# Threshold search by marks, sums on TensorE and two groups, with the weight quantisation on VectorE in its gaps

## The reference, cut to what matters

```
# layer 0, per batch: h = ctx (512 x 128), x' = layernorm(x)
sim = sum over heads of Q K^T / (sqrt(32) * 4)          # 512 x 512
k = int(512 * 0.3)                                      # 153
threshold = top_k(sim, k)[0][:, -1:]                    # the k-th largest of each row
A = sigmoid(sim) * (sim >= threshold)
A = (A + A^T) * 0.5
x = x + tanh(g_xattn[0]) * ((1 - gamma) * x' + gamma * A)
# layer 1: weights w_gate, w_up (2048 x 512), w_down (512 x 2048) are quantised in
# blocks of 32 (shared power of two, 1-bit mantissa, saturation at 6), then
out = (silu(q(z) @ q(w_gate)^T) * (q(z) @ q(w_up)^T)) quantised, @ q(w_down)^T
# layers 2 and 3 (attention; top-2 of 8 experts) are not touched
```

## Time and profile before

| | |
|---|---|
| median of 3 runs | 2155.13 us (2154.55 to 2155.16) |
| profiled execution, its time | 2153.45 us |
| its span on the core | 2151.7 us, mean granted TensorE clock 0.83 |
| DVE busy | 1576.6 us (73%) |
| PE busy | 1449.3 us (67%) |
| ACT busy | 959.3 us (45%) |
| POOL busy | 426.4 us (20%) |

### The profile page before, as it was taken

The page is one execution under the profiler, slowest core; times in us unless marked ns, Lnnn a source line. Parts: engine busy times, 40 slices in busy tenths (PEclk is TensorE's granted clock), DMA queues, the critical chain, the costliest instruction groups (busy, mean ns, idle before and its releaser), DMA issues.

```text
span 2151.7 us, 32048 instructions
## 1 busy us (share of the span) xinstructions
PE 1449.3 (67%) x10939; PEld 922.7 (43%) x11014; DVE 1576.6 (73%) x2526; ACT 959.3 (45%) x1591; POOL 426.4 (20%) x325
## 2 busy tenths in 40 slices
PE   4000051113767776889999770999999999999990
PEld 2000040012333332444444370677777777777760
DVE  4999999997888887888888453466666666666634
ACT  5787811123232223555545332455555555555520
POOL 3000003243000000666767606000000000000006
PEclk8555575556888887999999855899999999999995
DMA  9000030100000000000000007666666666666617
GB/s 354 9 0 0 0 118 0 78 0 25 0 0 0 0 0 0 2 1 2 2 2 1 2 0 273 226 227 233 227 225 232 227 226 229 229 227 229 228 61 234
DMA packets 86470, 222.09 MB, mean 103 GB/s; under 512 B 7424, under 2 KB 7680, under 8 KB 85888
## 3 DMA queue, kind: packets, MB, share of 16 engines
q1 hardware_dynamic: 80752, 204.37, 27.8%
q0 software_dynamic: 5120, 16.78, 2.3%
q10 hardware_dynamic: 528, 0.02, 0.0%
HBM read 184.44 MB, written 36.70 MB: 103 GB/s over the span
## 4 chain that ended last, share of the span: by engine, by line
PE 47%; DVE 7%; issue 4%; POOL 2%; ACT 0%; DMA 0%; POOLq 0%; DVEq 0%; ACTq 0%; SPq 0%
PE PS L1527 23%; PE PS L1546 11%; PE PS L1164 3%; DVE R L1017 2%; PE PS L1140 2%; PE PS L1150 2%; PE PS L1125 2%; DVE R L989 2%; PE PS L1139 1%; POOL R L1696 1%; PE PS L1412 1%; PE PS L1507 1%; PE PS L1115 1%; PE PS L1404 1%; DVE R L1021 1%
## 5 line engine op out<-in xcount | busy, mean ns | idle before, releaser
L1527 PE MATMUL PS<-R 128*128 128x256 f16 x4416 | 499.1, 273 | 1.1 <-ACT R L1583 1.1
L1527 PEld LDWEIGHTS PS<-R 128*128 128x128 f16 x4416 | 431.8, 98 | 66.8 <-issue 1.4
L1546 PE MATMUL PS<-R 128*128 128x512 f16 x1104 | 253.3, 379 | 0.2 <-DVE R L1656 0.2
L1234 DVE SCALAR_TENSOR_TENSOR R<-wring,R 128x1024 f16<-128x1024 f32 x184 | 221.3, 1223 | 27.5 <-ACT R L1229 24.3
L1092 ACT ACTIVATE R<-PS 128x512 f32<-128x512 f32 x256 | 151.6, 597 | 160.4 <-PE PS L1140 157.1
L989 DVE TENSOR_REDUCE R<-PS 128x1 f32<-128x512 f32 x256 | 167.4, 685 | 49.5 <-PE PS L1125 48.0
L399 ACT ACTIVATE R<-R 128x512 bf16<-128x512 f32 x256 | 181.0, 708 | 45.1 <-DVE R L443 45.1
L1229 ACT ACTIVATE R<-wring 128x1024 f16<-128x1024 f32 x184 | 188.9, 1050 | 23.8 <-DMA wring<-in_L_ffn_w_kernel_dram 21.3
L833 PE MATMUL PS<-R 128*128 128x512 bf16 x495 | 143.0, 439 | 78.1 <-DVE R L769 59.8
L1696 POOL DMA_INDIRECT R<-slot_out,posi x32 | 34.0, 1061 | 764.5 <-DMA slot_out<-R 755.1
L1648 DVE SCALAR_TENSOR_TENSOR R<-PS,R 128x512 f32<-128x512 f32 x92 | 63.5, 690 | 165.6 <-ACT R L1596 165.6
(11 more groups left out here) (221 smaller groups left out, 2508.9 us busy)
## 6 DMA issues: line engine op xcount, KB each, us to landing
wring<-in_L_ffn_w_kernel_dram SPq DMA_DIRECT2D x138, 512.0 KB, 4.3
R<-in_L_ffn_w_kernel_dram SPq DMA_DIRECT2D x46, 512.0 KB, 4.6
wring<-in_L_ffn_wo_kernel_dram SPq DMA_DIRECT2D x46, 512.0 KB, 5.1
R<-in_L_ffn_wo_kernel_dram SPq DMA_DIRECT2D x46, 512.0 KB, 5.0
slot_rows<-R SPq DMA_DIRECT2D x1, 11776.0 KB, 41.1
R<-slot_rows SPq DMA_DIRECT2D x23, 512.0 KB, 4.2
slot_out<-R SPq DMA_DIRECT2D x23, 512.0 KB, 3.0
X<-in_x_dram SPq DMA_DIRECT2D x4, 1024.0 KB, 9.0
```

The costliest lines, as they stand in the source:

```text
L1234: nc.vector.scalar_tensor_tensor(out=lo, in0=raw[c % RING], scalar=WSCALE, in1=hi, op0=ALU.mult, op1=ALU.subtract).then_inc(cut_lo, 1)
L1527: mm = nc.tensor.matmul(bank[2 * (j % 2) + m][:, g * SLOT:(g + 1) * SLOT], w[:, at:at + P], z[:, pz * 1024 + k * SLOT:pz * 1024 + (k + 1) ...
L1546: mm = nc.tensor.matmul(bank[6 + t], src[:, c * SLOT + t * P:c * SLOT + (t + 1) * P], w[:, at:at + D], start=(c == 0 and src is IH and pw ...
```

## The change

- The search step compares all 16 tiles on ACT. It writes the marks (`Sign`, +1, 0 or -1 in bf16) and takes no sum. The tiles are two groups of eight, and a half step `h` is one bit of one group: 64 half steps (`HALVES`) in place of 32 steps. `marks` holds eight tiles, the marks of one half step.
- PE adds the marks: eight matmuls of 128x256 with the identity for four tiles, which leave 64 partial sums per row in a bank. DVE reduces 8x64 to 8 counts (`tally`), and makes the next candidate of that group at once from two prepared values (`key`, `near`). The bits are 32 constants.
- Between two half steps DVE does one fifth of a weight unit (`dve_weights(v, u, k)`), 60 pieces in the first 60 half steps. The multiplication by the reciprocal, POOL's before, is now DVE's. PE's transposes and ACT's copies of a unit stand in the same sequence, after every fifth half step.
- The last count is of all 16 tiles: DVE writes the marks, PE adds them.
- The raw units are loaded from the start on through six slots. `A` now overwrites `SIM`, since the weights fill `R2` meanwhile.
- The keys stand in the apply part: `pe_keys(b)` ahead of the tiles of batch `b`, with POOL's subtraction and ACT's casts and copies to match, ACT's all after the sigmoids. The apply part uses six banks in place of eight.

```diff
         def act_search(act):
             act.wait_ge(sim_sb, NT)
-            def search(n):
-                act.wait_ge(cand_ready, n + 1)
-                act.wait_ge(act_counts, n * ACT_TILES + 1)
-                for t in range(DVE_TILES, NT):
-                    nc.scalar.activation(junk[:, t * S:(t + 1) * S], SIM[:, t * S:(t + 1) * S], ACT.Sign,
-                                         bias=cfloat[:, t:t + 1], scale=-1.0, accum_out=cnt[:, t:t + 1]).then_inc(act_counts, 1)
...
+            for h in range(HALVES):
+                act.wait_ge(cand_ready, h + 1)
+                for j in range(HALF):
+                    tile = h % 2 * HALF + j
+                    if j % 4 == 0 and h:
+                        act.wait_ge(fold_ps, 2 * h - 1 + j // 4)
+                    nc.scalar.activation(marks[:, j * S:(j + 1) * S], SIM[:, tile * S:(tile + 1) * S], ACT.Sign,
+                                         bias=cfloat[:, tile:tile + 1], scale=-1.0).then_inc(marked, 1)
+                if h >= 6 and (h - 6) % 5 == 0 and (h - 6) // 5 < 11:
+                    act_weights(act, (h - 6) // 5)
+            act_weights(act, 11)
+            act.wait_ge(raw_used, 12)
             with act.Fori(0, NT) as t:
                 nc.scalar.activation(SIG[:, bass.ds(t * S, S)], SIM[:, bass.ds(t * S, S)],
                                      ACT.Sigmoid).then_inc(sig_sb, 1)
+            for b in range(NB):
+                act_key_parts(act, b)
+                act_keys(act, b)
+
+        def pe_search(pe):
...
+            for h in range(HALVES + 2):
+                for q in range(2):
+                    pe.wait_ge(marked, h * HALF + 4 * q + 4)
+                    for c in range(8):
+                        mm = nc.tensor.matmul(bank[4 + h % 2][:, q * 256:(q + 1) * 256],
+                                              ident_b[:], marks.rearrange("p (t m) -> p t m", m=S)[:, 4 * q:4 * q + 4, c * 64:(c + 1) * 64],
+                                              start=(c == 0), stop=(c == 7))
+                    mm.then_inc(fold_ps, 1)
+                if h >= 5 and h % 5 == 0 and h <= 60:
+                    pe_weights(pe, h // 5 - 1)
...
+            def tally(h):
+                v.wait_ge(fold_ps, 2 * h + 2)
+                nc.vector.tensor_reduce(cnt[:, h % 2 * HALF:h % 2 * HALF + HALF],
+                                        bank[4 + h % 2].rearrange("p (t m) -> p t m", m=64), AX, ALU.add).then_inc(tallied, 1)
+                v.wait_ge(tallied, h + 1)
+
+            def search(h):
+                n, g = h // 2, slice(h % 2 * HALF, h % 2 * HALF + HALF)
+                tally(h)
+                nc.vector.tensor_scalar(keep[:, g], cnt[:, g], float(S - 2 * TOPK), -1.0, ALU.is_le,
+                                        ALU.mult).then_inc(keep_step, 1)
+                v.wait_ge(keep_step, h + 1)
...
+                if n < 31:
+                    nc.vector.scalar_tensor_tensor(out=cbits[:, g], in0=keep[:, g], scalar=bit[:, n:n + 1], in1=near[:, g],
+                                                   op0=ALU.bitwise_and, op1=ALU.bitwise_xor).then_inc(cand_ready, 1)
+                nc.vector.scalar_tensor_tensor(out=key[:, g], in0=keep[:, g], scalar=bit[:, n:n + 1], in1=key[:, g],
+                                               op0=ALU.bitwise_and, op1=ALU.bitwise_xor).then_inc(key_step, 1)
+                v.wait_ge(key_step, h + 5)
+                if n < 30:
+                    nc.vector.tensor_scalar(near[:, g], key[:, g], bit[:, n + 2:n + 3], None,
+                                            ALU.bitwise_xor).then_inc(near_step, 1)
...
+            for u in range(12):
+                for k in range(5):
+                    search(5 * u + k)
+                    dve_weights(v, u, k)
+            for h in range(60, HALVES):
+                search(h)
...
+            for h in range(HALVES, HALVES + 2):
+                for j in range(HALF):
+                    t = h % 2 * HALF + j
+                    if j % 4 == 0:
+                        v.wait_ge(fold_ps, 2 * h - 1 + j // 4)
+                    nc.vector.tensor_scalar(marks[:, j * S:(j + 1) * S], SIM[:, t * S:(t + 1) * S],
+                                            cfloat[:, t:t + 1], None, ALU.is_ge).then_inc(marked, 1)
...
+        def dve_weights(v, u, k):
...
+            if k == 0:
+                v.wait_ge(raw_in[raw_slot(u)], raw_loads(u))
...
                 nc.vector.tensor_reduce(wam, blocks(raw_u), AX, ALU.max, apply_absolute_value=True).then_inc(wf_step, 1)
...
+            elif k == 1:
+                wf(4)
+                nc.vector.tensor_tensor(blocks(wy), blocks(raw_u), spread(wri, n), ALU.mult).then_inc(raw_used, 1)
+                v.wait_ge(raw_used, u + 1)
+                nc.vector.tensor_scalar(wc.bitcast(I32), wy.bitcast(I32), EXPONENT, None,
                                         ALU.bitwise_and).then_inc(wq_step, 1)
+            elif k == 2:
+                wq(1)
                 nc.vector.tensor_scalar(wc, wc, 1.0, 1.5 * 2.0 ** 22, ALU.max, ALU.mult).then_inc(wq_step, 1)
+                wq(2)
+                nc.vector.scalar_tensor_tensor(out=wy, in0=wy, scalar=6.0, in1=wc, op0=ALU.min,
                                                op1=ALU.add).then_inc(wq_step, 1)
+            elif k == 3:
+                wq(3)
+                nc.vector.tensor_tensor(wy, wy, wc, ALU.subtract).then_inc(wq_step, 1)
+            else:
+                wq(4)
+                if u:
                     v.wait_ge(wtr_ps, 2 * u)
+                nc.vector.scalar_tensor_tensor(out=blocks(wb), in0=blocks(wy), scalar=-6.0, in1=spread(wsc, n),
                                                op0=ALU.max, op1=ALU.mult).then_inc(wb_ready, 1)
...
         def act_key_parts(act, b):
-            act.wait_ge(kt_ps, b * 2 + 1)
+            if b:
+                act.wait_ge(kt_ps, b * 2)
+            else:
+                act.wait_ge(fold_ps, 2 * HALVES + 4)
...
+        def sp_weights(sp):
+            for u in range(12):
+                if u >= 6:
+                    sp.wait_ge(raw_used, u - 3)
```

More of the change, by code:

```diff
@@ L23 @@
 EPS = 1e-5
-DVE_TILES = 8
-ACT_TILES = NT - DVE_TILES
+HALF = NT // 2
+HALVES = 64
+RAWS = 6
 QK_SCALE = float(HD) ** -0.5
@@ L112, in ints @@
             return R3[:, 5700 + 16 * k:5716 + 16 * k].bitcast(I32)
-        key, bit, cand, flip, cbits, keep, one = (ints(k) for k in range(7))
-        bits = [bit, ints(7)]
+        key, near, cand, flip, cbits, keep, one, gone = (ints(k) for k in range(8))
         cfloat = cbits.bitcast(F32)
         cnt = R3[:, 5700 + 16 * 8:5716 + 16 * 8]
-        junk = R3[:, 0:NT * S // 2].bitcast(BF16)
-        A = R2[:, 0:8192]
+        bit = R3[:, 5844:5876].bitcast(I32)
+        marks = R3[:, 6144:8192].bitcast(BF16)
+        A = R1[:, 0:8192]
         SIM = R1[:, 0:8192]
@@ L130, in bass_flamingo @@
         wpow = R3[:, 5184:5248]
-        wsc = [R3[:, 5248 + 64 * n:5312 + 64 * n] for n in range(2)]
-        wri = [R3[:, 5376 + 64 * n:5440 + 64 * n] for n in range(2)]
+        wsc = R3[:, 5248:5312]
+        wri = R3[:, 5376:5440]
         bz = R1[:, 8192:8704]
@@ L459, in dve_a @@
-            with v.Fori(0, 32, 2) as n:
-                search(n, 0)
-                search(n + 1, 1)
-            v.wait_ge(bit_step, 32 * 6 + 3)
+            nc.vector.tensor_copy(gone, key).then_inc(cand_ready, 2)
+            def tally(h):
[3 more added lines that the diff above has]
+                v.wait_ge(tallied, h + 1)
@@ L679, in pool_b_weights @@
-            pool_keys(pool, 3)
+            for b in range(NB):
+                pool_keys(pool, b)
             pool_selectors(pool)
         def pool_selectors(pool):
+            pool.wait_ge(a_ready, NT)
             nc.gpsimd.memset(sel, 0.0).then_inc(vo_step, 1)
@@ L710, in act_b_weights, with pe_weights, act_weights @@
-        def act_b_weights(act):
+        def pe_weights(pe, u):
+            pe.wait_ge(wb_ready, u + 1)
+            for h in range(2):
+                pe.wait_ge(wtr_sb, 2 * u + 1)
+                for n in range(8):
+                    at = ((n % 4) * D + (2 * h + n // 4) * P) if u < 8 else (8 * h + n) * P
+                    mm = nc.tensor.transpose(bank[h].bitcast(BF16)[:, n * P:(n + 1) * P], wb[:, at:at + P], ident_b[:])
+                mm.then_inc(wtr_ps, 1)
+        def act_weights(act, u):
@@ L711, in act_b_weights @@
             gu = WGU.rearrange("p (k o) -> p k o", k=4)
             dn = WDT.rearrange("p (c o) -> p c o", c=16)
[L714 to L724 removed]
+            if u == 0:
+                act.wait_ge(xs_zero, 16)
```

258 lines of the change are left out of this document (90 added, 168 removed).

## The result

The changed kernel takes 2071.38 us (median of 4 runs, 2069.66 to 2072.41). Beside it the kernel before took 2154.84 (4 runs, 2149.3 to 2155.16): a ratio of 0.9618, with a 95% interval of 0.9601 to 0.9635. The forecast was 2078.0 in a range of 2055 to 2115; it was 6.6 us too high. The profiled execution took 2070.64 us, 82.8 less than before's, with a span of 2068.5, 83.2 less.

The account below looks back on a forecast made before the run. Two long DVE-led stretches that don't overlap bound the kernel. Last mark 378.6 plus 59 gives norm factors at 437.6, 77.6 us earlier; 2153.45 - 77.6 = 2075.9 profiled, plus 1.7 for the median: 2078, range 2055 to 2115.

Parts of the forecast that it names:

- The last count: After the search: sums, count, DVE's marks of 16 tiles and small operations, putting masking 15.3 us after the last mark.
- The mark at 0.615: ACT's search half steps: one mark without its sum every 0.615 us, so 4.92 a half step and 314.9 for 64.
- bounds of 0.52 and 0.71: Mark-price rivals in ACT's search: 0.52, from the sigmoids, 2029 us, chance 0.05; 0.71, sum read free before, 2125, chance 0.07.
- The pairs of copies: ACT's two copies of a weight unit: 1.93 us together; eleven of twelve pairs inside the search, 20.4 us.
- the one stall: Search start: ACT waits 3 us (bounds 0 and 6) for a candidate because DVE must wait for unit 0's load.
- the last mark: End of ACT's marks in the search, forecast at 378.6 us: 40.3 + 314.9 + 20.4 + 3.
- Late candidates: Rival in the search: slow scaling pass makes DVE late, ACT stands 2.0 us a unit, 24 us, 2102; chance 0.18.
- the scaling pass: DVE's weight pass L628 in piece k = 2: forecast 1.26 us; 4.53 before while POOL multiplied.
- The rival by which PE holds the marks: Search: ACT waits for PE's sums, slowed by reading runs of 64 from four tiles; 2224 us at 0.45 a matmul; chance 0.05.
- The norm factors: The second layer's, ending the apply part: forecast 59 us after the last mark, at 437.6 where they were at 515.2.
- the first tile at +21.1: Start of the apply part: first tile 21.1 us after the last mark, behind ACT's casts, POOL's subtraction and PE's keys.

Follow-up runs that it names:

- the experiment with the sum: The changed kernel with ACT's marks taking a sum again, which nobody reads: 2117.67 us (single), 46.3 more.

## Why the prediction was right

**What ACT sets.** The mark at 0.615 was measured at 0.613, against bounds of 0.52 and 0.71; the experiment with the sum gives the difference to 0.71 as 0.09, on ACT's path in full. The Trainium skill's rule on the pointer (ScalarE: Activation LUTs, What ACT_TABLE_LOAD costs) would have given 0.614, and the trace agrees. The pairs of copies are 1.93 us, as read. ACT was the bound throughout but for the one stall, as counted, and the last mark ended at 378.0 where I had 378.6.

**DVE in the gaps.** The passes cost what the earlier trace rows show with POOL idle. The candidates were in time, from 70 to 350 us without one wait of ACT's. How much was spare is shown for the first piece of a unit only, where I had left out the cover that ACT's copies give. Late candidates, the likeliest rival, fell by the 1.22 us of the scaling pass. (Its own sum is 0.2 us a unit short: 3.5 late less 1.3 of slack leave 2.2, or 26 us in all, and not 2.0 and 24.) The cause that the rival named is real all the same; it only was not in this kernel, since nothing ran on POOL in the search. The kernels with the multiplication on POOL brought it back, and it took hold of another instruction than the one that I had priced.

**PE.** Eight matmuls of 256 columns took up to 1.89 us, as counted from a transpose of 128. That PE would stay at its low clock was a safe side and not what happened: part of the groups took 1.05. The runs of 64 out of four tiles cost nothing that shows. The rival by which PE holds the marks needed 0.38 us for a matmul; the slow ones take 0.23, and sums done twice held ACT for 6.5 us in all.

**The start.** The candidate that came late is the one for the fourth half step, behind 24 marks. The stall was 3.95 us where I had 3. The unit landed at 54.07 in place of 52.9; the rest was as counted. That it was the load is shown by the run in which it went ahead of the zeros.

**The last count.** I had 15.3 us from the last mark to masking, and it was 15.9. This agreement is luck, errors that offset each other. Two small operations, L526 and L528, took 1.17 and 1.07 in place of 0.17 each beside POOL's first subtraction, 1.9 us more. Against that, the last group of sums, at 388.98, took 1.05 us at the faster clock, where I had 2.1 with the hand-over, and DVE's mark was 0.41 us and not 0.45 (eight in 3.26): some 0.9 and 0.3 less.

**The keys and the apply part.** Here lies the miss. The norm factors came 55.6 us after the last mark where I had 59. I took POOL's subtraction at 4.7 and 5.2, between 3.44 and 6.15; it took 2.26 for the first, 3.35 for the second and 2.8 for the others. So POOL and the keys, by which I had the first tile at +21.1, were through before that, and what the tile waited for was DVE's masks (the row at 396.68, 1.06 us for L538): it started at +18.7, 2.8 us behind the start of masking, as before the change (276.70 to 279.49). Here the price and the path were both other than I had said; my sum for the path by the masks would have been 15.3 + 2.8 = 18.1. A batch took 7.95 us (405.46 to 413.41), not 8.5, and was set by PE with its keys, POOL being through in time. With the last mark 0.6 earlier this makes 4.0 of the 5.3 us between forecast and profiled execution; the other 1.2 or so came behind the factors, where I had counted nothing, and are too few to be told from the spread of the executions.

**What the sum did not say.** The forecast gave 77.6 us as one difference. The runs part it: the cheaper marks are no gain by themselves (80 us slower than before without the overlap), and the second group is what lets ACT run on while sum, count and candidate are made.

## What to carry to other kernels

Where two long stretches are each led by one engine, first ask which engine idles in both, and whether the dependent chain of one can be cut into two groups, so that the other's work fits between. After such a change read which engine has no idle time left and move single instructions from it to one that still waits: here 63 marks and one load brought 29 us more, to 2042.56 us, 5.1% under the kernel before. Work moved to an idle engine is not free by that alone: here POOL held DVE by more than the moved passes had cost it. Time the smallest instructions of the engine that is to be relieved beside the moved work, and not only the largest.

## What the runs showed of the hardware that I had not expected

- A VectorE operation on 7 or 8 elements a row took 3.09 us in place of 0.16 while GpSimd multiplied 2048 fp32 columns by the factors of their blocks (3.64 us); the operation on 7 ended within 0.02 us of GpSimd's. In the kernel before, the large pass L628 (4.53 us from 322.46) ended 1.07 us behind the end of GpSimd's, near its own 1.23: it too looks like a wait and then the usual work. Not all are held: a reduction out of PSUM and an operation on one column kept their 0.63 and 0.15 beside it. What decides between them was not tried. The Trainium skill (GPSIMD Engine Reference, Specifications) says that the two share their way to on-chip memory and that VectorE instructions in a 2-port mode or with two inputs contend. These rows agree that they contend; in them the wait lasts for nearly the rest of GpSimd's instruction, however small VectorE's is.
- Twice the matmuls in the search put its end back by 6.7 us only. PE was busy 218 of 280 us in place of 175 and its granted clock was 0.96 in place of 0.72, so that sixteen matmuls took 1.92 us where eight at the low clock had taken 1.87.
